# A float32 layer of two feed-forward halves around attention: probability sums with one chain of accumulating DMAs in place of two, and inputs of the projections loaded a chunk ahead

## The chip, the cores and the metric

The kernel is one launch on one core of a Trainium2 chip. The metric is device time in microseconds (us), median of several runs.

## The reference, cut to what matters

There are 2 sequences of 2048 tokens with 512 features, 16 heads of 32 features, and a hidden size of 2048. Everything is float32.

```python
x = x + 0.5 * ffn(layernorm(x))          # hidden = relu(x @ sign(up).T * up_scale); out = hidden @ sign(down).T * down_scale * output_scale
x = x + attention(layernorm(x))          # q, k, v = x @ w.T ; softmax(q @ k.T / sqrt(32)) @ v ; @ w_o.T
x = x + 0.5 * ffn(layernorm(x))          # the same weights again
```

## The kernel before

**Stages.** The 4096 tokens are cut into 8 chunks of 512, and x is held transposed (features on partitions). The first stage is the first feed-forward half; its result goes to HBM as `x_after_ffn` (`x1` in the code). The second stage, the projections (class `Qkv`), loads `x1` again, normalizes it and makes q, k and v, chunk by chunk; q, k and v go to HBM. The third stage is the attention (class `Attention`), 32 heads one after the other (16 heads of two sequences; `NH` is 32). The last stage is the output projection with the second feed-forward half. All instructions are written out in a fixed order for each engine, with semaphores between them; an engine that waits holds up everything behind it.

**Projections.** A chunk n has 12 tiles t (`NT`): four of q, four of k, four of v. A tile is 12 matmuls of TensorE (PE) into one of four banks (L553); ScalarE (ACT) copies the bank's high part out (L528, for v L530), VectorE (DVE) makes the low part (L517), and SyncE (SP) stores both. While chunk n is multiplied, chunk n+1 is normalized in steps of DVE (`vector_norm`, k from 0 to 17), ACT and PE. DVE takes steps 0 to 3 in front of tile 0, step 4 after tile 1, steps 5 to 8 after tile 2, step 9 after tile 5, steps 10 to 15 (with a reciprocal) after tile 6, and 16 and 17 after tile 8. PE has two matmuls of the norm (L141, L142) behind tile 1, which need step 3, and two behind tile 5. The buffers `x[0]` and `x[1]` take turns by chunk. SP loads the input for chunk n+1 at the top of its loop for chunk n, thus behind the last store of chunk n-1.

**First maxima.** Softmax needs the maximum of every row of scores. For each head, 64 blocks of 128x512 scores are made by PE in a bank (L806) and reduced by DVE (L737). Attention makes the maxima of head H+1 between the tiles of head H, but those of head 0 and the first 16 blocks of head 1, 80 blocks in all, are made in the projections. `FIRST_AT[n, t]` says how many blocks stand at tile t of chunk n: half of them in the middle of the tile's matmuls, the rest behind it. They use two banks in turn: PE makes block b only when DVE has read block b-2. DVE reads the blocks of a tile behind its norm steps there. Blocks need head 0's q, k and v on the chip, which SP loads after the store of tile 2 of chunk 4 (`att.load(sp, 0)`, seven DMAs, L679 and L681).

**Attention.** A head has 16 tiles kt of 128 keys by 2048 queries. For a tile PE makes four banks of scores (L802), ACT takes the exponential of each (L786) into one of 8 buffers `prob[kt % 8]`, and PE multiplies the tile by v (`out_tile`, L830). PE goes in groups of two tiles: 8 score matmuls and 8 maxima of the next head in turn, then the `out_tile`s of the group before. The denominators need the sum over all 16 tiles. It is made in two ways at once:

- POOL (GpSimd) adds the tiles in `pooled(H)` into `att_acc` (L710); the first add takes two tiles.
- The tiles in `moved(H)` are added into `att_dma_acc` by DMAs that POOL issues (L722 copies the first, L725 accumulates the others). There are `CHAINS` such accumulators, which take the moved tiles in turn.

Tiles in neither set are "direct": PE sums them with a matmul against ones in `out_tile` (L837). `Attention.move` waits, on POOL, for the tile's exponentials and for the DMA before it in its chain:

```python
pool.wait_ge(self.exp_done, UNITS * H + QC * (kt + 1))
if moves_to(H, kt) > 1:
    pool.wait_ge(self.dma_summed[x], 16 * (moves_to(H, kt) - 1))
```

POOL takes the tiles in order of kt, adds and DMAs in one queue. In group 2 of the next head (behind its tiles 4 and 5 of scores), PE sums the accumulators over the partitions (`sums`): 8 instructions for `att_acc` (L846) and 8 for each `att_dma_acc` (L851), behind waits for the last add and for the last DMA of each chain. ACT may write a buffer of `prob` again when the tile eight before has been multiplied and its add or its DMA is done (`tile_free`).

SP loads q, k and v of head H+2 when the head before H is wholly multiplied, early in head H, and then stores the output of head H-1 and moves its sums.

Of the kernel before, what the change touches and what calls it, by code (L numbers as in the profile page):

```python
# [17 lines left out]
NCH = TOK // CH  # L18
DT = D // P
HT = HID // P  # L20
KT = SEQ // P
QC = SEQ // CH
NH = BATCH * HEADS
# [429 lines left out]
NT, QR = 12, 4  # L453
# [134 lines left out]
SUMS_AFTER = 2  # L588
SUMS_AT, TURN_AT = QC * G * (SUMS_AFTER + 1), QC * 7 * G
SLOTS = UNITS + 2  # L590
CHAINS = 2
PER = 7 * 16
TURN = KT - LEAD + 1
NEG = 3
# [13 lines left out]


def pooled(H):  # L610
    return (0, 2, 4) if H == NH - 1 else tuple(range(0, KT, 2)) + ((KT - 1,) if H < NH - 2 else ())


def moved(H):
    return (1, 3, 5, 6, 7, 9, 10, 11) if H == NH - 1 else tuple(range(1, KT - 1, 2))


def direct(H):
    return tuple(kt for kt in range(KT) if kt not in pooled(H) and kt not in moved(H))


def adds_to(H, kt):

    return sum(len(pooled(h)) - 1 for h in range(H)) + max(1, pooled(H).index(kt))


def moves_to(H, kt):

    i = moved(H).index(kt)
    return sum(len(moved(h)[i % CHAINS::CHAINS]) for h in range(H)) + i // CHAINS + 1  # L630


def all_adds(H):
    return adds_to(H, pooled(H)[-1])


def all_moves(H, x):
    return moves_to(H, moved(H)[x::CHAINS][-1])


class Attention:
# [3 lines left out]
    def __init__(self, c, qk_parts, v_scr, head_out, ident, ones_sum):  # L645
# [16 lines left out]
        self.s_ready, self.exp_done, self.p_used = c.sem("att_s_ready"), c.sem("att_exp_done"), c.sem("att_p_used")  # L662
        self.summed, self.dma_summed = c.sem("att_summed"), [c.sem(f"att_dma_summed{x}") for x in range(CHAINS)]
        self.move_begun, self.t_ready = c.sem("att_move_begun"), c.sem("att_t_ready")
# [47 lines left out]
    def move(self, pool, H, kt):  # L712
        x = moved(H).index(kt) % CHAINS
        into = self.dma_acc[H % 2][x]
# [3 lines that stand above are left out]
        if moved(H).index(kt) < CHAINS:  # L718
            if H >= 2:
                pool.wait_ge(self.t_ready, H - 1)  # L720
            pool.sem_inc(self.move_begun, 1)
            self.nc.gpsimd.dma_start(into[:], self.prob[kt % PR][:]).then_inc(self.dma_summed[x], 16)  # L722
        else:
            pool.sem_inc(self.move_begun, 1)
            self.nc.gpsimd.dma_start(into[:], self.prob[kt % PR][:], accum_op=ALU.add).then_inc(self.dma_summed[x], 16)  # L725
# [45 lines left out]
    def tile_free(self, act, H, kt):  # L771
# [7 lines left out]
        elif old in moved(h):  # L779
            act.wait_ge(self.dma_summed[moved(h).index(old) % CHAINS], 16 * moves_to(h, old))  # L780

# [87 lines left out]
    def tensor_group(self, pe, H, u):  # L869
# [21 lines left out]
        if u == SUMS_AFTER and H > 0:  # L891
# [1 line left out]
            self.sums(pe, H - 1)  # L893


FIRST_AT = {**{(4, t): 2 for t in range(4, NT)}, **{(n, t): 1 for n in (5, 6) for t in range(NT)},
            **{(7, t): 4 for t in (0, 1, 2, 3, 4, 5, 8, 9, 10, 11)}}
FIRST_FROM = {}
for _n in range(4, NCH):
    for _t in range(NT):  # L900
        FIRST_FROM[_n, _t] = sum(k for at, k in FIRST_AT.items() if at < (_n, _t))
FIRST_TURN = (NCH - 1, 6)


def macaron_kernel(nc, xT, w_qT, w_kT, w_vT, w_oT, upT, downT, up_scale, down_scale, output_scale, outT):
    ctx = ExitStack()
    with ctx:
# [3 lines left out]
        def dram(n, shape, dt=F32):  # L911
            return nc.dram_tensor(n, shape, dt, kind="Internal").ap()

        x1 = dram("x_after_ffn", [P, DT, TOK])
# [13 lines left out]
        st = Stream(c, ones_mean)  # L928
# [18 lines left out]
        with nc.Block() as block:  # L947
            @block.sync
            def _(sp):
                st.load(sp, 0, xT)  # L950
                sp.dma_start(up_s[:], up_scale).then_inc(const_loaded, 16)
                sp.dma_start(down_s[:], down_scale).then_inc(const_loaded, 16)
                sp.dma_start(out_s[:], output_scale).then_inc(const_loaded, 16)
                for q in SIGN_ORDER[:6]:
                    signs1.load(sp, q)
                st.load(sp, 1, xT)
                for q in SIGN_ORDER[6:]:
                    signs1.load(sp, q)
                sp.wait_ge(signs1.made, 8)
                qkv.load_weights(sp, (w_qT, w_kT, w_vT))  # L960
                for n in range(NCH):
                    sp.wait_ge(ffn1.down_read, n + 1)
                    if n < NCH - 2:
                        st.load(sp, n + 2, xT)
                    else:
                        sp.wait_ge(st.stored, 16 * (n - NCH + 3))
                        st.load(sp, n + 2, x1)
                    ffn1.store(sp, n)
                sp.wait_ge(st.stored, 16 * NCH)

                for n in range(NCH):
                    if 1 <= n < NCH - 1:
                        sp.wait_ge(norm.dve, NV * (NCH + n + 1))
                        st.load(sp, NCH + n + 1, x1)
                    for t in range(NT):
                        qkv.store(sp, n, t)
                        if n == 4 and t == 2:
                            qkv.all_stored(sp, 4)
                            sp.wait_ge(att.ones_set, 2)
                            att.load(sp, 0)  # L980
                        if n == 4 and t == 6:
                            att.load(sp, 1)
                        if (n, t) == FIRST_TURN:
                            att.max_rows(sp, 0)
                qkv.all_stored(sp, NCH)

                for H in range(NH):
                    if H > 0:
                        att.head_free(sp, H)
                    if H + 2 < NH:  # L990
                        att.load(sp, H + 2)
                    if H == 0:
                        sp.dma_start(wo_raw[:], w_oT).then_inc(wo_loaded, 16)
                    if H == LAST - 1:
                        oproj.load(sp, 0)
                        st.load(sp, 2 * NCH, x1)
                    if H == LAST:
                        signs2.load(sp, 0)
                        oproj.load(sp, 1)
                    if H > 0:  # L1000
                        head_out.store_out(sp, H - 1)
                        head_out.move_sums(sp, H - 1)
                        head_out.store_inverse(sp, H - 1)
                    if H < LAST:
                        att.max_rows(sp, H + 1)

                sp.wait_ge(oproj.scaled, 2)
                signs2.load(sp, 4)
                signs2.load(sp, 1)
                head_out.store_out(sp, LAST)  # L1010
                signs2.load(sp, 5)
                sp.wait_ge(att.t_ready, NH)
                st.load(sp, 2 * NCH + 1, x1)
                head_out.move_sums(sp, LAST)
                signs2.load(sp, 2)
                head_out.store_inverse(sp, LAST)
                oproj.load(sp, 2)
                for q in SIGN_ORDER[5:]:
                    signs2.load(sp, q)
                sp.wait_ge(head_out.out_stored, 16 * QC * NH)  # L1020
                sp.wait_ge(head_out.inv_stored, 16 * NH)
                for n in range(NCH):
                    if 1 <= n < NCH - 2:
                        oproj.load(sp, n + 2)
                    sp.wait_ge(ffn2.down_read, n + 1)
                    if n < NCH - 2:
                        st.load(sp, 2 * NCH + n + 2, x1)
                    ffn2.store(sp, n)
                sp.wait_ge(st.stored, 16 * 2 * NCH)
# [30 lines left out]
            def _(dve):  # L1060
# [10 lines left out]
                for n in range(NCH):  # L1071
# [4 lines left out]
                    for t in range(NT):  # L1076
                        qkv.vector(dve, n, t)
                        for b in range(FIRST_AT.get((n, t), 0)):
                            att.first_block(dve, FIRST_FROM[n, t] + b)
# [75 lines left out]
            def _(pe):  # L1155
# [7 lines left out]
                for n in range(NCH):  # L1163
                    for t in range(NT):
                        if n == 0 and t == 1:
                            pe.wait_ge(ffn1.down_read, NCH)
                        first, count = FIRST_FROM.get((n, t), 0), FIRST_AT.get((n, t), 0)

# [72 lines left out]
```

## Time and profile before

| | |
|---|---|
| median of 3 runs | 3158.17 us (3157.16 to 3158.48) |
| the profiled execution | 3161.7 us, span 3159.7 us |
| TensorE busy | 2992.2 us, 95% |
| VectorE busy | 2037.9 us, 64% |
| ScalarE busy | 1613.2 us, 51% |
| GpSimd busy | 1330.5 us, 42% |
| mean granted TensorE clock | 0.979 |

The projections take about 520 to 905 us of the span, the attention about 905 to 2585 us. The busy shares are means over stages with different limits. A matmul's end is modelled and overlaps the next one, so its own duration (0.39 us) is longer than its pitch; the pitch is what counts.

### The profile page before, as it was taken

The numbers are of one execution on the slowest core, as the hardware profiler recorded it, in microseconds if no ns is written. First come the engines' busy times: TensorE is split into PE (matmuls) and PEld (weight loads), VectorE is DVE, ScalarE is ACT, GpSimd is POOL, SyncE is SP. The second block draws the span as 40 slices with busy tenths as digits, with TensorE's granted clock in tenths as the row PEclk, the third lists the DMA queues.
The fourth block names the chain that finished last, engine by engine and source line by source line (L and its number), as shares of the span: only waits on it lengthen the run. The fifth ranks groups of instructions, "written<-read, shape, count | busy, mean of one in ns | idle before, by whom it ended". The sixth has DMA issues, their size and how long they took to land.

```text
span 3159.7 us, 38839 instructions
## 1 busy us (share of the span) xinstructions
PE 2992.2 (95%) x14768; PEld 1974.2 (62%) x14768; DVE 2037.9 (64%) x3044; ACT 1613.2 (51%) x2851; POOL 1330.5 (42%) x489
## 2 busy tenths in 40 slices
PE   6999999877799999999999999999999889999998
PEld 4888887766565555555555555555555437888887
DVE  4555556646577777777877777777777335555552
ACT  5444443222146666666666666666666554333333
POOL 0000000000048878787888888787878610000000
PEclk9999999988899999999999999999999889999999
DMA  4110112444258887878788888888787763221200
GB/s 149 53 52 27 31 50 94 153 157 133 106 163 186 183 192 175 191 173 199 177 193 182 188 183 188 191 180 192 175 191 172 206 150 92 82 54 54 54 27 27
DMA packets 184891, 428.54 MB, mean 136 GB/s; under 512 B 89728, under 2 KB 90752, under 8 KB 148224
## 3 DMA queue, kind: packets, MB, share of 16 engines
q0 software_dynamic: 32400, 235.94, 32.2%
q1 hardware_dynamic: 152304, 190.11, 21.7%
q8 instruction: 116, 1.90, 0.2%
q14 instruction: 71, 0.58, 0.1%
HBM read 121.91 MB, written 67.63 MB: 60 GB/s over the span
## 4 chain that ended last, share of the span: by engine, by line
PE 72%; ACT 9%; DMA 7%; DVE 5%; issue 3%; POOL 3%; SPq 0%; ACTq 0%; DVEq 0%; POOLq 0%
PE bank L426 15%; PE bank L445 14%; PE bank L830 13%; PE bank L802 10%; ACT att_p L786 7%; PE bank L806 7%; PE bank L553 7%; DMA att_dma_acc<-att_p 4%; POOL att_acc L710 3%; PE bank L317 3%; DVE att_row_max L737 2%; PE bank L851 2%; DMA x<-x_after_ffn 1%; PE bank L846 1%; DVE norm_inv L108 1%
## 5 line engine op out<-in xcount | busy, mean ns | idle before, releaser
L737 DVE TENSOR_REDUCE att_row_max<-bank 128x1 f32<-128x512 f32 x2048 | 1258.6, 682 | 376.8 <-PE bank L806 372.7
L786 ACT ACTIVATE att_p<-bank 128x512 f32<-128x512 f32 x2048 | 1047.3, 623 | 590.5 <-PE bank L802 583.9
L710 POOL TENSOR_TENSOR att_acc<-att_acc,att_p 128x2048 f32<-128x2048 f32 x217 | 995.0, 4585 | 221.9 <-ACT att_p L786 217.6
L802 PE MATMUL bank<-att_q,att_k 98*128 98x512 f32 x2048 | 854.2, 419 | 29.8 <-ACT att_p L786 25.4
L806 PE MATMUL bank<-att_k,att_q 96*128 96x512 f32 x2048 | 817.3, 400 | 48.0 <-DVE att_row_max L737 28.6
L802 PEld LDWEIGHTS bank<-att_q,att_k 98*128 98x128 f32 x2048 | 385.4, 188 | 401.6 <-issue 208.4
L830 PE MATMUL bank<-att_p,att_v 128*32 128x512 f32 x4096 | 504.8, 611 | 0.0
L806 PEld LDWEIGHTS bank<-att_k,att_q 96*128 96x128 f32 x2048 | 391.1, 191 | 124.0 <-DVE att_row_max L737 36.3
L369 DVE TENSOR_TENSOR ffn_hid_lo<-ffn_hid,ffn_hid_hi 128x512 fp32r<-128x512 f32 x256 | 176.0, 688 | 431.1 <-ACT ffn_hid_hi L404 413.5
L426 PE MATMUL bank<-hi,ffn_up_w 128*128 128x512 f32 x1024 | 403.0, 394 | 20.2 <-DVE lo L122 15.2
L401 ACT ACTIVATE ffn_hid<-bank,up_s 128x512 f32<-128x512 f32 x256 | 175.9, 687 | 475.9 <-PE bank L426 475.3
L426 PE MATMUL bank<-lo,ffn_up_w 128*128 128x512 f32 x1024 | 402.3, 393 | 0.0
L445 PE MATMUL bank<-ffn_hid_hi,ffn_down_w 128*128 128x512 f32 x1024 | 399.6, 390 | 1.9 <-DVE ffn_hid_lo L369 1.9
L445 PE MATMUL bank<-ffn_hid_lo,ffn_down_w 128*128 128x512 f32 x1024 | 399.6, 390 | 0.0
L698 POOL MEMSET att_k<- 2x2048 f32 x3 | 5.3, 1800 | 900.9 <-PE bank L445 505.6
L830 PEld LDWEIGHTS bank<-att_p,att_v 128*32 128x32 f32 x4096 | 108.5, 110 | 246.4 <-ACT att_p L786 132.7
L426 PEld LDWEIGHTS bank<-hi,ffn_up_w 128*128 128x128 f32 x1024 | 194.6, 190 | 63.4 <-DVE lo L122 12.5
L426 PEld LDWEIGHTS bank<-lo,ffn_up_w 128*128 128x128 f32 x1024 | 194.6, 190 | 41.2
L445 PEld LDWEIGHTS bank<-ffn_hid_hi,ffn_down_w 128*128 128x128 f32 x1024 | 192.7, 188 | 43.0 <-DVE ffn_hid_lo L369 2.4
L445 PEld LDWEIGHTS bank<-ffn_hid_lo,ffn_down_w 128*128 128x128 f32 x1024 | 192.7, 188 | 40.6
L710 POOL TENSOR_TENSOR att_acc<-att_p,att_p 128x2048 f32<-128x2048 f32 x32 | 146.4, 4574 | 76.0 <-ACT att_p L786 76.0
L404 ACT ACTIVATE ffn_hid_hi<-bank,up_s 128x512 fp32r<-128x512 f32 x256 | 174.5, 682 | 0.0
(89 smaller groups left out, 2237.5 us busy)
## 6 DMA issues: line engine op xcount, KB each, us to landing
att_dma_acc<-att_p POOLq DMA_DIRECT2D x225, 1024.0 KB, 7.6
x<-x_after_ffn SPq DMA_DIRECT2D x16, 1024.0 KB, 7.4
att_q<-q_hi SPq DMA_DIRECT2D x64, 256.0 KB, 4.3
att_k<-k_hi SPq DMA_DIRECT2D x64, 256.0 KB, 8.9
x<-xT SPq DMA_DIRECT2D x8, 1024.0 KB, 7.0
x_after_ffn<-x_out SPq DMA_DIRECT2D x8, 1024.0 KB, 9.5
q_hi<-qkv_o_hi SPq DMA_DIRECT2D x32, 256.0 KB, 2.0
q_lo<-qkv_o_lo SPq DMA_DIRECT2D x32, 256.0 KB, 2.3
```

What stands on the lines that cost most here:

```text
L369: nc.vector.tensor_tensor(self.hid_lo[:, ht % RING, :], self.hid[:, ht % RAW, :], f32(self.hid_hi[:, ht % RING, :]), ALU.subtract).then_in ...
L401: nc.scalar.activation(self.hid[:, ht % RAW, :], self.up_ps[ht % 2][:], ACT.Relu, scale=self.vecs["up"][:, ht:ht + 1])
L404: nc.scalar.activation(self.hid_hi[:, ht % RING, :], self.up_ps[ht % 2][:], ACT.Relu, scale=self.vecs["up"][:, ht:ht + 1]).then_inc(self.u ...
L426: ins = nc.tensor.matmul(self.up_ps[ht % 2][:], signs.up[:, ht // 4, dt, ht % 4 * P:(ht % 4 + 1) * P], part[N % 2][:, dt, :], start=(dt == ...
L445: ins = nc.tensor.matmul(self.down_ps[dt][:], signs.down[:, h, dt * P:(dt + 1) * P], part[:, h % RING, :], start=(h == 0 and i == 0), stop ...
L553: ins = self.nc.tensor.matmul(self.out_ps[t % QR][:], left, right, start=(dt == 0 and (a, b) == (0, 0)), stop=(dt == DT - 1 and (a, b) == ...
L710: self.nc.gpsimd.tensor_tensor(self.acc[H % 2][:], a[:], self.prob[kt % PR][:], ALU.add).then_inc(self.summed, 1)
L737: self.nc.vector.tensor_reduce(self.row_max[odd][:, qt, q:q + 1], m[:], axis=AX.X, op=ALU.max).then_inc(self.m_read, 1)
L786: self.nc.scalar.activation(self.prob[kt % PR][:, q * CH:(q + 1) * CH], self.s_ps[S_BANK[kt * QC + q]][:], ACT.Exp, scale=SCALE).then_inc( ...
L802: self.nc.tensor.matmul(self.s_ps[S_BANK[i]][:], self.k_st[H % NB][0:KM, kt * P:(kt + 1) * P], self.q_st[H % NB][0:KM, q * CH:(q + 1) * CH ...
L806: self.nc.tensor.matmul(m[:], self.q_st[T % NB][0:KQ, qt * P:(qt + 1) * P], self.k_st[T % NB][0:KQ, q * CH:(q + 1) * CH], start=True, stop ...
L830: ins = self.nc.tensor.matmul(self.o_ps[rows, :], self.v_st[H % NB][:, kt, :], self.prob[kt % PR][:, q * CH:(q + 1) * CH], start=(kt == 0) ...
```

## The change

It has two parts. In the projections the input of chunk n+2 is loaded at the top of SP's loop for chunk n (before, that of chunk n+1, from n = 1 on), and the 80 first blocks stand elsewhere: chunk 4 has 8, two at each of tiles 8 to 11 (before 16, two at each of tiles 4 to 11), chunks 5 and 6 have 16 each, two at tiles 0, 3, 6 and 9 and one elsewhere (before 12 each, one a tile); chunk 7 keeps its 40.

In the attention there is one chain of DMAs. In a head below 30, POOL has 10 tiles (9 adds) in place of 9 (8 adds), and the chain has 6 in place of 7. In head 30 POOL keeps 8 tiles, the chain has 6 in place of 7, and 2 tiles are direct in place of 1. In head 31 POOL keeps 3 tiles, the chain has 5 in place of 8, and 8 tiles are direct in place of 5.

```diff
-CHAINS = 2
+CHAINS = 1
...
 def pooled(H):
-    return (0, 2, 4) if H == NH - 1 else tuple(range(0, KT, 2)) + ((KT - 1,) if H < NH - 2 else ())
+    if H == NH - 1:
+        return (0, 2, 4)
+    return (0, 2, 3, 5, 6, 8, 10, 11) + ((13, 15) if H < NH - 2 else ())
...
 def moved(H):
-    return (1, 3, 5, 6, 7, 9, 10, 11) if H == NH - 1 else tuple(range(1, KT - 1, 2))
+    return (1, 5, 7, 9, 11) if H == NH - 1 else (1, 4, 7, 9, 12, 14)
...
-FIRST_AT = {**{(4, t): 2 for t in range(4, NT)}, **{(n, t): 1 for n in (5, 6) for t in range(NT)},
+FIRST_AT = {**{(4, t): 2 for t in range(8, NT)}, **{(n, t): 1 if t % 3 else 2 for n in (5, 6) for t in range(NT)},
             **{(7, t): 4 for t in (0, 1, 2, 3, 4, 5, 8, 9, 10, 11)}}
...
                 for n in range(NCH):
-                    if 1 <= n < NCH - 1:
+                    if n < NCH - 2:
                         sp.wait_ge(norm.dve, NV * (NCH + n + 1))
-                        st.load(sp, NCH + n + 1, x1)
+                        st.load(sp, NCH + n + 2, x1)
```

## Rows read from the trace of the kernel before

**Rows 1.** The page's 40 slices of the span, busy and clock in tenths.

```profile
PE   6999999877799999999999999999999889999998
PEclk9999999988899999999999999999999889999999
```

**Rows 2.** Busy time in stretches: a chunk of projections, a head of attention.

```profile
640.00:680.00 40.00, 35.66 (x148) 28.95 (x148) 23.76 (x26) 11.40 (x16) 0.00 (x0) 0.92 0.44 158
1539.70:1591.00 51.30, 50.38 (x282) 27.23 (x281) 39.77 (x69) 33.41 (x67) 41.75 (x15) 1.00 0.80 185
```

**Rows 3.** The chain that ended last, projections: start, us, what.

```profile
639.77 1.24 DVE norm_work L83
...
656.81 16.38 PE bank L553 x72
...
680.39 1.24 DVE norm_work L83
...
694.01 7.79 DMA att_v<-v_rows
...
748.58 1.24 DVE norm_work L83
...
779.80 4.35 PE bank L553 x12
...
797.85 1.24 DVE norm_work L83
```

**Rows 4.** TensorE in order of time; in brackets its idle time before, and for whom.

```profile
642.96 0.79 PE L141 MATMUL bank<-norm_sum_hi,ones_mean 128*128 128x512 f32 x1 [5.17 <-DVE norm_sum_lo L89]
701.84 0.79 PE L806 MATMUL bank<-att_k,att_q 96*128 96x512 f32 x1 [8.80 <-DMA att_v<-v_rows]
724.16 0.80 PE L806 MATMUL bank<-att_k,att_q 96*128 96x512 f32 x1 [8.23 <-DVE att_row_max L737]
779.30 0.50 PE L806 MATMUL bank<-att_k,att_q 96*128 96x512 f32 x1 [3.90 <-DVE att_row_max L737]
```

**Rows 5.** VectorE in order of time, behind tile 6 of chunk 5.

```profile
770.12 0.69 DVE L517 TENSOR_TENSOR qkv_o_lo<-bank,qkv_o_hi 128x512 fp32r<-128x512 f32 x1 [1.56 <-ACT qkv_o_hi L528]
...
778.56 0.68 DVE L737 TENSOR_REDUCE att_row_max<-bank 128x1 f32<-128x512 f32 x1
...
780.35 2.35 DVE L122 TENSOR_TENSOR lo<-norm_work,hi 128x1024 fp32r<-128x1024 f32 x2
```

**Rows 6.** The chain that ended last, in a head of attention.

```profile
1535.47 0.86 PE bank L846 x8
1536.33 1.72 PE bank L851 x16
```

**Rows 7.** GpSimd in order of time, a head and the end of head 30.

```profile
1565.40 9.30 POOL L710 TENSOR_TENSOR att_acc<-att_acc,att_p 128x2048 f32<-128x2048 f32 x2 [0.83 <-ACT att_p L786]
...
2480.24 0.86 POOL L725 DMA_DIRECT2D att_dma_acc<-att_p  x1
...
2485.66 0.88 POOL L725 DMA_DIRECT2D att_dma_acc<-att_p  x1
```

**Rows 8.** ScalarE: eight exponentials each, tiles 12 and 13, then 14 and 15.

```profile
1557.04 4.03 ACT L786 ACTIVATE att_p<-bank 128x512 f32<-128x512 f32 x8 [1.98 <-PE bank L802]
1563.25 4.03 ACT L786 ACTIVATE att_p<-bank 128x512 f32<-128x512 f32 x8 [2.18 <-PE bank L802]
```

**Rows 9.** Landing of all 142 accumulating DMAs (L725) from 1100 to 2860 us.

```profile
DMA to landing us min/median/max: 6.8/7.3/12.5
```

**Rows 10.** DMA issues: KB, us to landing. Windows 1523:1524, 1545:1546.2, and at 2508.26.

```profile
att_dma_acc<-att_p POOLq DMA_DIRECT2D x1, 1024.0 KB, 9.1
att_dma_acc<-att_p POOLq DMA_DIRECT2D x1, 1024.0 KB, 6.9
att_dma_acc<-att_p POOLq DMA_DIRECT2D x1, 1024.0 KB, 4.5
```

**Rows 11.** The queue of SyncE early in a head, first of its seven loads.

```profile
1523.09 0.79 SPq L679 DMA_DIRECT2D att_q<-q_hi  x2
```

## The prediction

> **What bounds the kernel now.** I first read the page's slices [rows 1]: TensorE is full nearly everywhere; the one dip, to 7 tenths with a lower granted clock, is the projections. Then the table by stretch [rows 2]: a chunk of projections has 4.3 us of idle TensorE and a granted clock of 0.92; a head of attention has 50.4 busy us in 51.3, at clock 1.00, with GpSimd at 41.8 and the DMA engines at 0.80. So two things matter. In the projections, TensorE waits; the chain and TensorE's timeline say for what [rows 3, 4]. In the attention TensorE is the bound, work taken from it comes back as time, but only while nothing else has a longer cycle. GpSimd with its DMAs is the next candidate, and the change loads it.
>
> **Projections, the loads.** The load is issued behind the last store of the chunk before; VectorE's steps 0 to 3 wait for it, and TensorE stands 5.17 us in front of the mean's matmuls [rows 4]. From one such start of step 0 to the next are 680.39 - 639.77 = 40.6 us [rows 3]. A matmul has a pitch of 16.38 / 72 = 0.2275 us [rows 3], so the 148 of a chunk are 33.7 us, and 6.9 us are lost: the stall and the slower clock behind it. How much is clock is seen behind another stall: twelve matmuls took 4.35 us in place of 2.73 [rows 3], 1.6 us. The new load has a whole chunk of time; steps 0 to 3 then run in the tail of the chunk before, where VectorE has nothing else from step 17 on. Chunks 1 to 3 gain 3 x 6.9 = 20.7 us. The load now stands ahead of the stores of tile 0, whose slots are needed four tiles (11 us) later: no cost.
>
> **Chunk 4** took 748.58 - 680.39 = 68.2 us. It had the same stall, 8.8 us for head 0's loads, and 8.2 us for block reads behind VectorE's norm steps [rows 4]. Afterwards the blocks begin at tile 8, by the pitch some 10 us after the last of these loads is issued, and that one takes 7.79 us [rows 3]: the wait goes. A new one comes. Behind tile 6 VectorE takes from its low part (770.12) to the end of step 15 (778.56) 8.4 us [rows 5]. With 0.8 us ahead of it, the low part of tile 7 (0.6), steps 16 and 17 (2.35) and the read itself (0.7) the first block is read 12.9 us after tile 6. TensorE wants its bank for the third block, in the middle of tile 9, after 2.5 x 2.73 + 2 x 0.23 = 7.3 us: it stands 5.6 us. So 33.7 + 8 x 0.23 + 5.6 + 1.6 = 42.7 us, a gain of 25.5.
>
> **Chunks 5 and 6** took 49.3 us each [rows 3], of which the load's stall and 3.90 us for the reads behind the norm steps [rows 4]. They lose the first stall but get 4 blocks more (0.9). With one block behind tile 7 following two at tile 6, TensorE needs a bank one tile sooner: it arrives 3.0 us after tile 6, and the read ends at 0.8 + 8.4 + 0.7 = 9.9: 6.9 us in place of 3.9. Likewise the second block of tile 3 waits for the read of tile 2's, which stands behind steps 5 to 8: by the same walk 3.7 us, and 1.6 for the clock. 33.7 + 16 x 0.23 + 6.9 + 1.6 + 3.7 + 1.6 = 51.2: a loss of 1.9 us each. Chunk 7 is unchanged. **Projections in all: -20.7 - 25.5 + 3.8 = -42 us** (-21 if the stores held up behind head 0's loads delay ScalarE in chunk 4, -50 if the walk's stalls are too long).
>
> **Attention, TensorE.** One accumulator less takes eight of the 16 L851 instructions, 0.86 us a head [rows 6]. If TensorE stays the bound, the head goes from 51.3 to 50.5 us. Heads 30 and 31 get four direct tiles, each with eight more instructions of the L846 kind, 0.86 us [rows 6]: +3.4.
>
> **Attention, GpSimd and the chain.** This is the step that decides. Before, a chain has every second moved tile, four tiles apart, and GpSimd's idle time ends with ScalarE, as in [rows 7]: no DMA wait binds. Now each move waits for the one before it, in GpSimd's own queue, so all later adds wait too. Moves are at tiles 1, 4, 7, 9, 12, 14 and again 1. Tile 14's exponentials follow tile 12's by 1563.25 - 1557.04 = 6.2 us [rows 8], while an accumulating DMA takes 6.8 us at best, 7.3 in the median [rows 9]. In the first heads tile 14's move therefore starts late, tile 15's add and the next head's move of tile 1 later, and the lag is carried on. GpSimd's cycle when it lags: one DMA and one add take 2485.66 - 2480.24 = 5.42 us [rows 7]; a second add is 9.30 / 2 = 4.6. Intervals with two adds (1 to 4, 4 to 7, 9 to 12) take about 10.0 us, more than a landing. Intervals with one add (7 to 9, 12 to 14, 14 to 1) take the landing L. With 0.1 off for the copy's shorter issue, **the cycle is 29.9 + the three L.** With L = 6.9 it is 50.6, just over TensorE's new 50.5; with 7.3 it is 51.8, over the present one.
>
> What is L? The one of tile 7 falls in a calm stretch: 6.9 [rows 10], I take 7.1. The others move, by the lag, into the start of the next head, where SyncE issues seven loads [rows 11]. The copy issued there took 9.1 us, alone 4.5 [rows 10], and the longest of all took 12.5 [rows 9]. So tile 12's has between 6.9 and 9, I take 7.5; tile 14's between 7.3 (it misses the loads) and 12 (it gives them half of the engines for its whole length), I take 10, 3 more than alone where the copy had 4.6 more. Cycle: 29.9 + 7.1 + 7.5 + 10 = 54.5 us. TensorE waits for the last DMA in `sums`, 17 to 18 us into the next head; the chain's last landing begins near 4 to 10 us there and gains 2 to 4 us a head, so after about 4 heads TensorE is held. That leaves 27 heads at 54.5 - 51.3 = +3.2: **+86 us**, and 4 heads at -0.86: -3. TensorE's stall is once a head, and its slower clock afterwards is hidden by the same lag. Heads 30 and 31 +3.4 - 1.7 = +2.
>
> The Trainium skill (DMA: Bandwidth & Descriptors, Bandwidth and "Queues, rings and completion order") says that each DMA engine takes the queues in turn, a packet from each. The copy's 9.1 against 4.5 us [rows 10] agrees; by equal turns the accumulate in the window would take about 12 us, which is the upper end above.
>
> **Sum:** -42 + 86 - 3 + 2 = +43 us on a span of 3159.7 (the run 3161.7, the median of the runs 3158.17, 3.5 less). On the median: 3201 us.
>
> **Rivals.** (a) *The chain never binds*: TensorE's 0.86 us a head come back. -42 - 32 x 0.86 + 3.4 = -66: 3092 us. For it: the DMAs are fewer (six for seven) and never overlap one another, so landings may be the 4.5 of the copy rather than 7.3. Against it: 6.8 is the minimum of 142 [rows 9]. The Trainium skill (DMA: Bandwidth & Descriptors, "Anatomy of one DMA") gives about 2.0 us + bytes / 436e3 for a DMA of this queue, 4.4 us for 1 MB, by which the chain would always be in time. The copy's 4.5 agrees; the accumulates' 6.8 to 7.3 do not, and the measurement decides. Chance 0.13. (b) *The chain binds at its calm pace*: the loads fall on tile 1's copy, which has 9.95 us anyway, and L is 6.9 to 7.3: cycle 50.6 to 51.8, attention -18 to +17, in all 3098 to 3133 us. Chance 0.17. (c) *Equal shares in the load window*: L of tiles 12 and 14 are 8.3 and 12; cycle 29.9 + 7.1 + 8.3 + 12 = 57.3, 27 x 6.0 = +162, in all 3277 us. Chance 0.18. (d) *Only the loads of chunks 1 to 3 give something*, because head 0's loads, still ahead of the stores in SyncE's queue, hold up chunk 4 as before: 3201 + 21 = 3222 us. Chance 0.04. The side is decided at a cycle of 51.3 + 42 / 27 = 52.9 us.
>
> **How the numbers follow.** The forecast, a cycle of 53 to 56 us, has 0.48: 3158 to 3240. A measurement of this kernel tells 0.2%, 6.3 us, from no change. Faster is (a), (b) and a corner of the forecast: 0.31. Within 0.2%: cycles of 52.7 to 53.1, 0.05. Slower: 0.64. The range goes from 3098, above (a), to 3278, which takes in (c) but not its worse half.
>
> **What would show it.** Right: GpSimd idle ahead of L725 at tiles 9 and 14 and L722 at tile 1, with no exponential as releaser; TensorE idle ahead of L846 or L851 once a head, some 3 to 4 us; `head_total` (L228) 53 to 56 us apart in place of 51.3; in the projections no L141 stall in chunks 1 to 6, a stall of 5 to 6 us at chunk 4's tile 9 and of 7 us behind tile 7 of chunks 5 and 6. Wrong: a head of 50.5 us with GpSimd's waits ending on ScalarE, which is (a); or landings of 7 us everywhere.

## The result, and the profile after

The changed kernel takes 3364.61 us (median of 4 runs, 3363.66 to 3366.45), the kernel before 3158.32 us in the same comparison. The ratio is 1.0655 (95% interval 1.0636 to 1.0673): 206 us slower. The forecast was 3201 us with a range up to 3278. The side was right, the size was not. The profiled execution took 3366.45 us with a span of 3364.4, so the spans differ by 204.7 us.

The page of the changed kernel, the span in 40 slices, answers to [rows 1]; below it stand the page's lines on the chain that ended last and on one group of the costliest instructions (busy us, mean ns | idle before and its releaser).

```profile
PE   6999999987989898898989889898988698999999
PEclk9999999988999999998989999899999898999999
...
PE 43%; DMA 29%; POOL 12%; issue 10%; DVE 3%; ACT 2%; SPq 0%; POOLq 0%; ACTq 0%; DVEq 0%
...
L727 POOL DMA_DIRECT2D att_dma_acc<-att_p x159 | 138.4, 870 | 265.4 <-issue 238.4
```

The dip of the projections is gone, and in its place TensorE has a gap in every head of the attention. DMAs and GpSimd together are 41% of the chain. GpSimd stood 238 us ahead of its own DMA issues, with no exponential as releaser: by the code that leaves the wait for the DMA before, and the run with two chains below shows it.

Line numbers from `moved` on are two higher than before (L725 is L727, L737 is L739, L802 is L804, L851 is L853); those ahead of `pooled` (L141, L228) are the same.

Two stretches of the changed kernel, a piece of the projections and one head from its first DMA to the next head's, answer to [rows 2] (columns: stretch, length, busy us of PE, PEld, DVE, ACT, POOL, granted clock, DMA share, GB/s).

```profile
640.00:680.00 40.00, 39.91 (x176) 32.59 (x175) 30.11 (x32) 12.02 (x18) 0.00 (x0) 1.00 0.67 200
1528.20:1587.30 59.10, 52.52 (x277) 28.09 (x273) 40.05 (x68) 33.82 (x66) 46.22 (x15) 0.93 0.67 143
```

The projections now have 39.9 busy us in 40 at clock 1.00. The head takes 59.1 us in place of 51.3, with the DMA engines less busy than before (0.67 for 0.80): on the mean of the head they aren't full, since GpSimd's transfers stand one behind the other.

ScalarE's copies of the sums (L228), one a head, split the difference. These are the first and the second of the changed kernel, and three at its end.

```profile
932.89 0.60 ACT L228 ACTIVATE head_total<-bank 128x512 f32<-128x512 f32 x1
998.53 0.60 ACT L228 ACTIVATE head_total<-bank 128x512 f32<-128x512 f32 x1
...
2661.58 0.59 ACT L228 ACTIVATE head_total<-bank 128x512 f32<-128x512 f32 x1
2745.60 0.60 ACT L228 ACTIVATE head_total<-bank 128x512 f32<-128x512 f32 x1
2792.14 0.59 ACT L228 ACTIVATE head_total<-bank 128x512 f32<-128x512 f32 x1
```

Before, the first stood at 973.11, the last three at 2463.61, 2538.33 and 2587.75. So up to the first copy the change gains 40.2 us. The 29 heads after it take 1728.7 us in place of 1490.5, 59.6 a head in place of 51.4: +238.2. The last two take 9.3 more and 2.9 less. Together -40.2 + 238.2 + 6.4 = +204.4, the difference of the spans.

GpSimd's timeline shows a head (answers to [rows 7]).

```profile
1528.24 0.60 POOL L724 DMA_DIRECT2D att_dma_acc<-att_p  x1 [4.67 <-issue]
1528.85 4.57 POOL L712 TENSOR_TENSOR att_acc<-att_p,att_p 128x2048 f32<-128x2048 f32 x1
1533.57 4.58 POOL L712 TENSOR_TENSOR att_acc<-att_acc,att_p 128x2048 f32<-128x2048 f32 x1
1538.09 0.87 POOL L727 DMA_DIRECT2D att_dma_acc<-att_p  x1
1538.73 9.59 POOL L712 TENSOR_TENSOR att_acc<-att_acc,att_p 128x2048 f32<-128x2048 f32 x2
1548.27 0.85 POOL L727 DMA_DIRECT2D att_dma_acc<-att_p  x1
1548.88 4.88 POOL L712 TENSOR_TENSOR att_acc<-att_acc,att_p 128x2048 f32<-128x2048 f32 x1
1555.68 0.87 POOL L727 DMA_DIRECT2D att_dma_acc<-att_p  x1 [1.91 <-issue]
1556.29 9.62 POOL L712 TENSOR_TENSOR att_acc<-att_acc,att_p 128x2048 f32<-128x2048 f32 x2
1565.85 0.87 POOL L727 DMA_DIRECT2D att_dma_acc<-att_p  x1
1566.46 4.88 POOL L712 TENSOR_TENSOR att_acc<-att_acc,att_p 128x2048 f32<-128x2048 f32 x1
1574.83 0.87 POOL L727 DMA_DIRECT2D att_dma_acc<-att_p  x1 [3.49 <-issue]
1575.44 4.88 POOL L712 TENSOR_TENSOR att_acc<-att_acc,att_p 128x2048 f32<-128x2048 f32 x1
1587.32 0.60 POOL L724 DMA_DIRECT2D att_dma_acc<-att_p  x1 [7.01 <-issue]
```

Where two adds stand between two DMAs (1528.24, 1538.09, 1548.27; 1555.68, 1565.85), GpSimd never waits. Where one add does, it waits 1.91, 3.49 and 7.01 us, for the DMAs of tiles 7, 12 and 14. Every later add waits with it.

### The profile page after: what moved, and what is told of

The parts are those of the page before. It is cut to its first block, busy times and chain, and to the rows that moved or that the text cites. A ratio compares the mean times of both kernels' runs of the same rounds, so it can differ in the third digit from the quotient of the medians.

```text
span 3364.4 us, 38353 instructions
## 1 busy us (share of the span) xinstructions
PE 3045.9 (91%) x14544; PEld 1994.2 (59%) x14544; DVE 2050.7 (61%) x3044; ACT 1625.6 (48%) x2851; POOL 1459.5 (43%) x485
## 4 chain that ended last, share of the span: by engine, by line
PE 43%; DMA 29%; POOL 12%; issue 10%; DVE 3%; ACT 2%; SPq 0%; POOLq 0%; ACTq 0%; DVEq 0%
DMA att_dma_acc<-att_p 29%; PE bank L426 14%; PE bank L445 13%; POOL att_acc L712 11%; PE bank L553 7%; PE bank L317 2%; PE bank L832 2%; PE bank L804 2%; PE bank L808 1%; ACT att_p L788 1%; DVE norm_inv L108 0%; PE bank L141 0%; PE bank L853 0%; DVE norm_work L118 0%; DMA x_out<-downT 0%
## 5 line engine op out<-in xcount | busy, mean ns | idle before, releaser
L739 DVE TENSOR_REDUCE att_row_max<-bank 128x1 f32<-128x512 f32 x2048 | 1271.2, 684 | 618.6 <-PE bank L808 614.6
L788 ACT ACTIVATE att_p<-bank 128x512 f32<-128x512 f32 x2048 | 1058.6, 616 | 814.7 <-PE bank L804 636.3
L712 POOL TENSOR_TENSOR att_acc<-att_acc,att_p 128x2048 f32<-128x2048 f32 x247 | 1175.3, 4758 | 18.7 <-ACT att_p L788 5.4
L804 PE MATMUL bank<-att_q,att_k 98*128 98x512 f32 x2048 | 888.3, 436 | 151.6 <-ACT att_p L788 145.1
L808 PE MATMUL bank<-att_k,att_q 96*128 96x512 f32 x2048 | 846.3, 414 | 46.7 <-DVE att_row_max L739 38.4
L804 PEld LDWEIGHTS bank<-att_q,att_k 98*128 98x128 f32 x2048 | 403.3, 197 | 549.4 <-ACT att_p L788 237.2
L832 PE MATMUL bank<-att_p,att_v 128*32 128x512 f32 x4096 | 524.3, 631 | 0.0
L808 PEld LDWEIGHTS bank<-att_k,att_q 96*128 96x128 f32 x2048 | 409.8, 200 | 125.8 <-DVE att_row_max L739 45.7
L727 POOL DMA_DIRECT2D att_dma_acc<-att_p x159 | 138.4, 870 | 265.4 <-issue 238.4
L445 PEld LDWEIGHTS bank<-ffn_hid_lo,ffn_down_w 128*128 128x128 f32 x1024 | 192.6, 188 | 40.5
```

The costliest lines, as they stand in the source:

```text
L445: ins = nc.tensor.matmul(self.down_ps[dt][:], signs.down[:, h, dt * P:(dt + 1) * P], part[:, h % RING, :], start=(h == 0 and i == 0), stop ...
L712: self.nc.gpsimd.tensor_tensor(self.acc[H % 2][:], a[:], self.prob[kt % PR][:], ALU.add).then_inc(self.summed, 1)
L739: self.nc.vector.tensor_reduce(self.row_max[odd][:, qt, q:q + 1], m[:], axis=AX.X, op=ALU.max).then_inc(self.m_read, 1)
L788: self.nc.scalar.activation(self.prob[kt % PR][:, q * CH:(q + 1) * CH], self.s_ps[S_BANK[kt * QC + q]][:], ACT.Exp, scale=SCALE).then_inc( ...
L804: self.nc.tensor.matmul(self.s_ps[S_BANK[i]][:], self.k_st[H % NB][0:KM, kt * P:(kt + 1) * P], self.q_st[H % NB][0:KM, q * CH:(q + 1) * CH ...
L808: self.nc.tensor.matmul(m[:], self.q_st[T % NB][0:KQ, qt * P:(qt + 1) * P], self.k_st[T % NB][0:KQ, q * CH:(q + 1) * CH], start=True, stop ...
```

## The experiments

The comparisons of each group of runs were made on one chip; the kernel before took 3153.4, 3157.1 and 3155.1 us on them, so the ratios are what to compare. A run of a single execution has no interval.

**The two parts by themselves.** First the projections' part alone: both edits in the projections, the attention as before.

```diff
 FIRST_AT = ... (as changed)
-                    if 1 <= n < NCH - 1:
+                    if n < NCH - 2:
                         sp.wait_ge(norm.dve, NV * (NCH + n + 1))
-                        st.load(sp, NCH + n + 1, x1)
+                        st.load(sp, NCH + n + 2, x1)
```

> Only the projections' part of the change (loads a chunk ahead, first blocks moved), the attention as before. Theory: the two parts add up. The projections gain the 41 us that the changed kernel's trace shows (its first DMA of the attention is issued at 869.5 in place of 910.0 us), heads stay at 51.3 us: 3117 us. Rival, that a part of the gain is given back where the attention starts (head 0's maxima now ready later): 3125 to 3135 us.

3115.87 us, ratio 0.9875 (0.9854 to 0.9896), by the ratio 39 us under the kernel before. The theory holds, the rival falls.

Then the attention's part alone: `CHAINS`, `pooled` and `moved` as changed, the projections as before.

> Only the attention's part (one chain of six, POOL ten), the projections as before. Theory: the whole loss is here, heads at about 59 us: 3365 + 41 = 3405 us, within 8. Rival, that the projections' new end set the lag going or sets its phase: heads under 57 us and below 3370 us.

3398.26 us (one execution), 1.078 of the kernel before there; 1.0655 and the 0.013 that the projections' part gives make 1.0785. The parts add up, and the attention's part is the whole loss. Its heads take 59.1 us.

**Is it the chain or the ninth add?** The changed kernel with two chains for the same six tiles.

```diff
-CHAINS = 1
+CHAINS = 2
```

> The changed kernel with two chains again that take the six moved tiles in turn; GpSimd keeps its ten tiles. Theory (the wait for the DMA before, in GpSimd's queue, is the cost): in one chain the moves are now at least five tiles apart, the waits go, TensorE is the bound with its 51.3 us a head: 3117 + 3 for the direct tiles of heads 30 and 31 = 3120 us. Rival (the ninth add, 4.6 us a head more of GpSimd): GpSimd is still late, heads of 54 us or more, over 3200 us.

3148.75 us, ratio 0.998 (0.997 to 0.999). The rival falls: with the same nine adds the heads take 52.4 us, and no DMA issue waits for the one before. The theory fell short by some 30 us, about 1 a head. TensorE's waits from 1100 to 2400 us in this run (us in total, times, longest) say where they are:

```profile
PEld bank L804 <- DMA att_q<-att_neg_lo: 45.3, 25, 3.3
...
PE bank L804 <- DMA att_q<-att_neg_lo: 22.6, 25, 2.4
```

The 22.6 us of TensorE's own waits (the weight loads' overlap them) over 25 heads are 0.9 a head: at the start of a head TensorE waits for the row of maxima, an 8 KB DMA. It now runs beside tile 12's DMA: in one head, issued at 1955.24, 1.2 us behind that one, it landed at 1961.44, that one at 1961.64; tile 14's was issued 4 us after it. That is 6.2 us from issue (6.17 in the median of 25 heads), where the median was 2.4 us in the kernel before. That the two accumulators are the reason is read from these times; no run moves the row's DMA alone.

**What makes the waits long?** The changed kernel with SyncE's seven loads of q, k and v moved behind the move of the sums, some 20 us later in the head.

```diff
-                    if H + 2 < NH:
-                        att.load(sp, H + 2)
+                    if H == 0:
+                        att.load(sp, 2)
...
                         head_out.move_sums(sp, H - 1)
+                        if H + 2 < NH:
+                            att.load(sp, H + 2)
                         head_out.store_inverse(sp, H - 1)
```

> The changed kernel, but the seven loads of head H+2 are issued behind the move of the sums (some 20 us later in the head) from head 1 on. Theory (the loads of q, k and v share the DMA engines with tile 12's and 14's DMAs and make these two long, 9.0 and 12.5 us in place of 7.4): the three single-add intervals come to 7.4 us each, a cycle of 30.2 + 22.2 = 52.4, up to 55 if the loads now lengthen tile 4's or 7's interval: 3175 to 3250 us. Rival (these intervals are long for another reason, such as GpSimd's own work or TensorE's stall): 3350 us or more.

3231.45 us (one execution), heads of 54.6 us. The intervals from one DMA issue of GpSimd to the next, worked out from the start times of all of them from 1100 to 2500 us (23 to 26 heads), are the measured form of the prediction's sum:

| interval, tiles | adds in it | predicted | changed kernel: mean (range) | loads later: mean (range) |
|---|---|---|---|---|
| 1 to 4 | 2 | 9.9 | 9.88 (9.83 to 9.93) | 9.90 (9.86 to 9.93) |
| 4 to 7 | 2 | 10.0 | 10.15 (10.11 to 10.18) | 11.13 (10.26 to 12.24) |
| 7 to 9 | 1 | 7.1 | 7.80 (7.39 to 9.71) | 7.86 (7.42 to 9.69) |
| 9 to 12 | 2 | 10.0 | 10.14 (10.08 to 10.18) | 10.13 (10.09 to 10.18) |
| 12 to 14 | 1 | 7.5 | 11.03 (8.04 to 13.54) | 7.87 (7.42 to 9.32) |
| 14 to 1 | 1 | 10 | 10.27 (8.39 to 13.40) | 7.74 (7.40 to 9.18) |
| cycle | 9 | 54.5 | 59.3 | 54.6 |

With the loads elsewhere the intervals behind tiles 12 and 14 fall to 7.9 and 7.7 us, and that of tile 4, whose DMA now has the loads beside it, grows by 1 us. So of the 8 us that a head lost, 4.7 go with the place of the loads, and the rest is the time of 7.7 to 7.9 us from issue to issue, which a single add doesn't cover. The rival falls. SyncE's stores of the head's output are not what makes the DMAs long: here they are in flight beside tile 12's DMA for 4.2 us of its flight in the mean (from 1100 to 2300 us), and it lands in 7.20 us in the mean.

**The projections' edits one by one.** The loads ahead alone:

> The kernel before with only the loads of the projections a chunk ahead; blocks and attention as before. Theory (each of the six boundary stalls costs 6.9 us, but in chunk 4 head 0's loads and in chunks 5 and 6 the block reads take part of it back): chunks 1 to 3 gain 20.7, chunks 4 to 6 about 6 each where no other stall grows, together 21 to 40 us: a ratio of 0.987 to 0.993. Rival (the blocks' move is what gains in chunk 4, and the boundary stalls of chunks 4 to 6 turn into block waits): 21 us, 0.993.

3117.55 us, ratio 0.9871 (0.9854 to 0.9888): the upper end of what the theory said, as much in time as both edits together. In its trace TensorE still stands 11.18 us in chunk 4 for head 0's loads:

```profile
676.80 0.79 PE L806 MATMUL bank<-att_k,att_q 96*128 96x512 f32 x1 [11.18 <-DMA att_v<-v_rows]
```

The move of the first blocks alone:

> The kernel before with only the first blocks moved. Theory: chunk 4 loses the wait for head 0's loads (8.8 us) and a wait for block reads, together some 17 us less with the 5 us of the new wait, chunks 5 and 6 get 8 us each more (four blocks more, the tile-3 and tile-7 waits): -25 + 6.9 + 16 = about 0, between -10 and +5 us. Rival (the move gains by itself): -15 us or more.

3159.38 us, ratio 1.0005 (0.9994 to 1.0016): about nothing, as the theory said. The rival falls: from first tile to first tile chunk 4 takes 51.0 us in place of 68.4, chunks 5 and 6 take 58.2 and 56.0 in place of 48.8 and 50.5, so that they give back 14.9 of the 17.4 us.

**A spacing with two adds everywhere.** If a cycle is the sum of its intervals, each the longer of a landing and its adds, then five moves three tiles apart leave no interval with one add. GpSimd gets an eleventh tile for it.

```diff
-    return (0, 2, 3, 5, 6, 8, 10, 11) + ((13, 15) if H < NH - 2 else ())
+    return (0, 2, 3, 5, 6, 8, 9) + ((11, 12, 14, 15) if H < NH - 2 else ())
...
-    return (1, 5, 7, 9, 11) if H == NH - 1 else (1, 4, 7, 9, 12, 14)
+    return (1, 5, 7, 9, 11) if H == NH - 1 else (1, 4, 7, 10, 13)
```

> The changed kernel with five moves, three tiles apart (1, 4, 7, 10, 13), still in one chain; GpSimd has 11 tiles (10 adds), so that two adds stand in every interval between moves. Theory (a cycle is the sum of the intervals, each the longer of a landing and its adds): 5 x 10.1 = 50.5 us, as long as TensorE's; the interval in the window of the seven loads is 11 to 12.5 in place of 10.1: heads of 51 to 53 us, in all 3110 to 3170 us where the kernel before takes 3158. Rival (a single chain is too slow at any spacing, since landings grow to the 59 us cycle): heads over 56 us, over 3260 us.

3102.33 us, ratio 0.9824 (0.9806 to 0.9843): better than the theory said, under both kernels and under the projections' part alone. Its page has GpSimd at 9 tenths in nearly every slice of the attention, and its timeline from 1100 to 2300 us has no wait for a DMA:

```profile
POOL 0000000000079999999999999999999500000000
```

```profile
1906.99 0.87 POOL L727 DMA_DIRECT2D att_dma_acc<-att_p  x1
1907.60 9.61 POOL L712 TENSOR_TENSOR att_acc<-att_acc,att_p 128x2048 f32<-128x2048 f32 x2
1917.16 0.84 POOL L727 DMA_DIRECT2D att_dma_acc<-att_p  x1
1917.76 9.56 POOL L712 TENSOR_TENSOR att_acc<-att_acc,att_p 128x2048 f32<-128x2048 f32 x2
1927.26 0.88 POOL L727 DMA_DIRECT2D att_dma_acc<-att_p  x1
```

The five intervals there are 9.90, 10.17, 10.17, 10.16 and 10.16 us in the mean, 50.6 together, and the longest of all 116 is 10.43: in this rhythm no DMA takes longer than its two adds, not even in the window of the loads (the longest landing is 9.75 us). One reason is where that window falls. The loads stand beside the end of tile 13's DMA and beside the copy of tile 1, which lands in 8.7 us in the mean from 1100 to 2300 us, where the changed kernel has them beside accumulating DMAs. GpSimd and TensorE have the same cycle. The run changes two things at once, five moves for six and even intervals for uneven ones, and no run tells them apart.

The same with SyncE's loads moved as above:

> The same with the seven loads issued behind the move of the sums. Theory: wherever the loads fall, one or two intervals of two adds are 11 in place of 10.1 us: heads of 51 to 52.5 us, about as the run without this (within 20 us). Rival (the loads' old place is what binds a single chain): at least 30 us less than it.

3207.45 us, ratio 1.0157 (1.0139 to 1.0174). Both expectations fell. Here the loads lengthen an interval (7 to 10 is 12.7 us), and they come too late: TensorE waits for them once a head, 24 times in the stretch. Its waits from 1100 to 2400 us:

```profile
PE bank L804 <- DMA att_v<-v_rows: 63.7, 24, 3.9
...
POOL att_dma_acc L727 <- DMA att_dma_acc<-att_p: 54.3, 23, 3.1
```

The maxima of head H+2 begin at tile 12 of head H, and the last of the loads, issued 3 us behind the first, takes 12.9 us in one head (12.2 in the median). The DMA of tile 7, beside these loads, lands in 12.1 us in the mean, longer than its two adds: even intervals alone are not enough, the loads' place counts too.

**Is one chain worth anything?** Five even moves with `CHAINS = 2`:

> Five even moves with two chains in place of one. Theory (with every interval at 10.1 us no wait for the DMA before binds, so the second chain only gives TensorE its 0.86 us a head back to do): 27 us slower than the one-chain form, 3129 us where that took 3102. Rival (one chain still costs something at this spacing): within 10 us of it or faster.

3121.24 us, ratio 0.9889 (0.9875 to 0.9904), 0.65% over the one-chain form: 20 us where 27 were expected. The heads take 51.3 us against 50.6. So most of TensorE's 0.86 us a head do come back once no wait stands in their way; GpSimd's own cycle of 50.6 us, then without a wait, leaves no room for the rest.

Five even moves in one chain with the first blocks where the kernel before had them:

> Five even moves in one chain, the loads ahead, but the first blocks where the kernel before had them. Theory: as the two single runs of the projections' parts gave equal times (3116 and 3118 us, with and without the move of the blocks), the move of the blocks gives nothing once the loads are ahead: 3102 within 6 us. Rival: the earlier end of the chunk-4 stalls helps, 3115 us or more without the move.

3109.86 us, ratio 0.9855 (0.9838 to 0.9871), against 0.9824 (0.9806 to 0.9843) with the blocks moved. Neither expectation held, and the two intervals just overlap. The traces show where the move acts. The first DMA of the attention is issued at 873.23 us without it and at 869.55 with it, and in the two runs with the old attention at 874.78 and 868.65: the projections end 4 to 6 us earlier. With the old attention the heads give this back (the last copy of the sums stands at 2545.20 without the move and at 2545.12 with it); whether any of it stays with five even moves isn't settled.

## Why the prediction was wrong

**The projections: right.** -42 us stood there, the trace shows -40.2 up to the first copy of the sums, the part alone 39. The stalls came where and as long as the walk had them. TensorE in order of time in the changed kernel, chunks 4 to 6 (answers to [rows 4]):

```profile
685.80 0.79 PE L808 MATMUL bank<-att_k,att_q 96*128 96x512 f32 x1 [5.05 <-DVE att_row_max L739]
712.89 0.50 PE L808 MATMUL bank<-att_k,att_q 96*128 96x512 f32 x1 [3.75 <-DVE att_row_max L739]
734.28 0.80 PE L808 MATMUL bank<-att_k,att_q 96*128 96x512 f32 x1 [6.87 <-DVE att_row_max L739]
765.15 0.50 PE L808 MATMUL bank<-att_k,att_q 96*128 96x512 f32 x1 [3.75 <-DVE att_row_max L739]
786.52 0.80 PE L808 MATMUL bank<-att_k,att_q 96*128 96x512 f32 x1 [6.87 <-DVE att_row_max L739]
```

Predicted were 5.6 at chunk 4's tile 9, and 3.7 and 6.9 twice. No L141 stall is left in chunks 1 to 6. The lengths of the chunks came too: 33.7 us for chunks 1 to 3 as forecast, 43.5 for 42.7 in chunk 4, 52.3 and 51.8 for 51.2 in chunks 5 and 6. What the sum did not say is that the loads alone give as much in the whole time; up to the first DMA of the attention (910.02 us before) they give 35.2 us, both edits 40.5.

**The attention: the mechanism was right, three sizes were not.** The structure of the cycle, three intervals of two adds and three of one, is the measured one; 29.9 us stood for the first three, 30.2 were measured.

The step that failed is "What is L?". Its three L were 7.1 + 7.5 + 10 = 24.6 us; measured are 7.8 + 11.0 + 10.3 = 29.1, so the term was 4.5 us a head too small, and 3.5 of them are tile 12's. The prediction took the landing alone as the interval. The trace of before had a calm landing of 6.9 us [rows 10]; from the issue of tile 7's to the next are at least 7.39 us, so half a microsecond of hand-over was missing in each. And it put tile 12's DMA for the most part ahead of the window of the loads. Its text gives no working for that place; in its rows the loads begin 13 us ahead of the sums that wait for the last landing (1523.09 and 1536.33, [rows 11, 6]). SyncE's queue in the changed kernel, the first of the seven loads and the stores behind them:

```profile
1507.47 0.80 SPq L681 DMA_DIRECT2D att_q<-q_hi  x2
...
1514.47 9.84 SPq L234 DMA_DIRECT2D attention_out<-head_raw  x4
```

Tile 12's DMA was issued at 1506.63, tile 14's at 1518.10, and the copy of tile 1 at 1528.24. The loads began 20.8 us ahead of that last issue: tile 12's DMA had the loads, tile 14's the last of the loads (they had landed by 1522.38) and the stores. In other heads tile 14's had most of the loads, so either of the two is long (8.0 to 13.5 and 8.4 to 13.4 us). The loads lie that much earlier because TensorE does not only stand in `sums` before that point. ScalarE in the changed kernel, tiles 4 and 5 of the head:

```profile
1516.80 4.23 ACT L788 ACTIVATE att_p<-bank 128x512 f32<-128x512 f32 x8 [4.37 <-DMA att_dma_acc<-att_p]
```

It waited 4.37 us for the buffer of the old tile 12, whose DMA hadn't landed (`tile_free`). The prediction did not name this wait; it had only the one in `sums`. TensorE stands in `sums` as well, ahead of L853 (answers to [rows 6]):

```profile
1527.69 1.94 PE L853 MATMUL bank<-att_dma_acc,ones_sum 128*32 128x512 f32 x8 [2.91 <-DMA att_dma_acc<-att_p]
...
1586.77 1.94 PE L853 MATMUL bank<-att_dma_acc,ones_sum 128*32 128x512 f32 x8 [5.25 <-DMA att_dma_acc<-att_p]
```

Of the two ways in which the chain holds TensorE, the one that the prediction did not name is the larger. The waits of the changed kernel from 1100 to 2600 us (us in total, times, longest):

```profile
ACT att_p L788 <- DMA att_dma_acc<-att_p: 139.4, 40, 7.8
PE bank L804 <- ACT att_p L788: 99.0, 64, 5.7
PE bank L853 <- DMA att_dma_acc<-att_p: 50.4, 18, 6.2
```

TensorE waits 99 us ahead of scores, for a bank that ScalarE has not yet read, and 50 us in `sums`; in the kernel before the first is 22 us in the same stretch, and none in `sums` is among the longer ones.

The account: 29 heads at +8.2 us are +238 where 27 at +3.2 and 4 at -0.86 (+83) stood, 155 us short. 27 x 5.1 = 138 of them are the cycle (59.6 for 54.5). The other 17 are that TensorE is held from the second head on, and not after about 4: from the first copy of the sums to the second are 65.6 us (4.6 of them are a subtraction that GpSimd makes once, behind tile 9 of head 1: that interval took 14.71 us for 10.14). The last two heads cost 6.4 in place of 2, the projections gave 40.2 in place of 42: 6 more. Together 161, and the forecast was 3364.6 - 3201 = 163.6 us short.

**The rivals.** (a), the chain never binds, fell by the timeline. (b), its calm pace, is what the run with the loads later comes near to, and even there 7.7 to 7.9 us stand in the place of 6.9 to 7.3. (c), equal shares in the window of the loads, with 57.3 us, was nearest and still under the measured 59.3: it gave tile 12 only 8.3 us. (d) fell: chunk 4 gained 24.9 us (68.4 to 43.5, first tile to first tile).

**What a landing costs.** The two means of 11.0 and 10.3 us beside the loads are 7.9 and 7.7 with the loads elsewhere. The Trainium skill (DMA: Bandwidth & Descriptors, "Queues, rings and completion order") says that a DMA engine takes its queues in turn, packet by packet. By that a DMA of GpSimd slows down while SyncE's are in flight, and these means agree. The Trainium skill (the same page, "Anatomy of one DMA") fits a DMA of GpSimd's queue with about 2.0 us and bytes / 436e3, 4.4 us for 1 MB. The copy agrees (4.5 us alone [rows 10]), the accumulates don't: 6.8 us at least [rows 9].

## What to carry to other kernels

A chain of DMAs whose waits stand in an engine's queue has a cycle of its own: add up its intervals, each the longer of the engine's work in it and the landing with its hand-over (half a microsecond here), and compare the sum, not the busy time, with the cycle of the engine that is the bound. Leave no interval in which the work is shorter than the landing: here a head went from 59.3 to 50.6 us by five even moves in place of six uneven ones, though GpSimd had one add more. Whether six moves could be had at that pace wasn't tried, and with the loads at another place the five even ones took 54.4. And place such a chain against the other queues' transfers only after asking who else waits for its landings, since those waits shift the whole pattern.

## What the runs showed of the hardware that was not expected

An 8 KB DMA of SyncE took 6.2 us in the median when a 1 MB accumulating DMA of GpSimd had been issued 0.8 to 1.2 us ahead of it (the changed kernel with two chains), 2.4 us in the kernel before, and 1.85 us where the DMA before had landed (five even moves, loads later: one landed at 1723.67, the row's was issued at 1724.03), and TensorE waited for it 0.9 us a head. A 1 MB accumulating DMA landed in 7.2 us beside SyncE's stores and in 12.1 beside its seven loads. GpSimd's DMA issue (0.87 us in the trace) holds the next add up by 0.61 to 0.64 us only, start to start. An accumulating DMA of 1 MB took 6.8 us in a calm stretch, 2.3 more than the plain copy of the same bytes.
